# Attention with scores, softmax and values in one loop, without the running maximum

## The reference

```python
xn = _layernorm(x)                       # x: 2 x 8192 x 1024
q, k, v = xn @ Wq, xn @ Wk, xn @ Wv      # 1024 x 1024 each
scores = where(causal, -inf, q @ k.T)
s = softmax(scores / sqrt(1024)) @ v
g = silu(ffn(xn))                        # gate, up: 1024 -> 3072, down: 3072 -> 1024, integer weights
x = x + s * g
```

## Time and profile before

| | us |
|---|---|
| median of 2 runs | 2159.85 (2154.26 to 2165.43) |
| the profiled execution | 2145.53 |
| its span, on core 7, the slowest | 2143.8 |
| spans of the eight cores | 2132.1 to 2143.8 |
| attention, first to last matmul, on core 7 | about 1404 to 2126 |

### The profile page before, as it was taken

One profiled execution on the slowest core, in us unless ns is written; L12 is line 12 of the kernel. 1 busy time (PEld: TensorE's weight loads), 2 busy tenths in 40 slices (PEclk: granted clock), 3 DMA queues, 4 the chain that ended last, 5 costly groups with the idle time before them and its releaser, 6 DMA issues.

```text
span 2143.8 us, 24577 instructions; the slowest of 8 cores (2132.1 to 2143.8 us)
## 1 busy us (share of the span) xinstructions
PE 1677.2 (78%) x8544; PEld 797.7 (37%) x8544; DVE 534.8 (25%) x1356; ACT 551.3 (26%) x842; POOL 87.3 (4%) x149
## 2 busy tenths in 40 slices
PE   0232499999999986799989998966778687878875
PEld 0222344444444443344434443323333333333332
DVE  3000033443443342111001110033323242341430
ACT  0242543444344333011001110022222222221321
POOL 0000000000000000000000000000000000001000
PEclk9955599999999998899999999988889999989988
DMA  9999333342433331433102330077787685765834
GB/s 194 199 217 192 107 136 138 138 156 102 155 138 141 115 118 61 120 76 79 40 1 56 73 79 10 1 248 222 234 258 236 217 273 200 244 235 185 295 138 157
DMA packets 165751, 320.66 MB, mean 150 GB/s; under 512 B 105088, under 2 KB 111232, under 8 KB 143104
## 3 DMA queue, kind: packets, MB, share of 16 engines
q0 software_dynamic: 29968, 151.00, 24.6%
q1 hardware_dynamic: 124144, 149.20, 22.6%
q10 hardware_dynamic: 11520, 18.88, 2.5%
HBM read 283.41 MB, written 60.82 MB: 161 GB/s over the span
## 4 chain that ended last, share of the span: by engine, by line
PE 65%; DMA 18%; ACT 5%; another core or an unknown queue 4%; issue 3%; DVE 2%; ACTq 1%; SPq 1%; DVEq 0%; POOL 0%; POOLq 0%
PE psBC L405 10%; DMA vbuf<-vv_s 9%; PE psD L592 8%; PE psA L550 8%; PE psA L435 5%; PE psD L435 5%; PE psA L667 4%; PE psBC L800 4%; PE psD L800 4%; PE psD L560 4%; PE psBC L560 4%; PE psBC L461 3%; DMA kbuf<-kT_s 3%; DMA wst<-wu 2%
## 5 line engine op out<-in xcount | busy, mean ns | idle before, releaser
L405 PE MATMUL psBC<-xns,wk_b 128*128 128x512 bf16 x1024 | 225.3, 381 | 1.3 <-ACT xns L381 1.3
L250 PE MATMUL psA<-ident_b,wst 128*128 128x128 bf16 x576 | 69.5, 295 | 189.9 <-DMA wst<-wg 86.9
L550 PE MATMUL psA<-xnq,wgu 128*128 128x512 bf16 x768 | 175.9, 383 | 27.5 <-DMA wgu<-wuT_s 27.5
L800 PE MATMUL psBC<-vbuf,pT 128*128 128x512 bf16 x512 | 138.5, 419 | 70.7 <-DMA vbuf<-vv_s 63.8
L592 PE MATMUL psD<-wdT_b,hact 128*128 128x512 bf16 x768 | 170.0, 381 | 21.4 <-ACT g_b L601 17.7
L360 DVE TENSOR_SCALAR xnr<-xkb,mvall,rstdall 128x1024 bf16<-128x1024 f32 x80 | 61.6, 810 | 500.5 <-PE psA L372 498.4
L667 PE MATMUL psA<-kbuf,qT 128*128 128x512 bf16 x608 | 143.0, 393 | 25.7 <-DMA kbuf<-kT_s 17.6
L800 PE MATMUL psD<-vbuf,pT 128*128 128x512 bf16 x576 | 143.1, 395 | 6.0 <-DMA vbuf<-vv_s 6.0
L405 PEld LDWEIGHTS psBC<-xns,wk_b 128*128 128x128 bf16 x1024 | 100.6, 98 | 123.2 <-issue 3.7
L775 ACT ACTIVATE pT<-psA 128x1024 bf16<-128x1024 bf16 x72 | 69.5, 976 | 261.6 <-PE psA L763 261.6
L250 PEld LDWEIGHTS psA<-ident_b,wst 128*128 128x128 bf16 x576 | 52.9, 133 | 206.2 <-issue 206.1
(11 more groups left out here) (83 smaller groups left out, 1677.3 us busy)
## 6 DMA issues: line engine op xcount, KB each, us to landing
vbuf<-vv_s POOLq DMA_DIRECT2D x72, 1024.0 KB, 5.8
kbuf<-kT_s SPq DMA_DIRECT2D x40, 1024.0 KB, 9.8
xkb<-xk SPq DMA_DIRECT2D x16, 2048.0 KB, 10.9
kbufX<-kT_s SPq DMA_DIRECT2D x32, 1024.0 KB, 13.6
kT_s<-kst POOLq DMA_DIRECT2D x16, 1024.0 KB, 5.7
vv_s<-vst POOLq DMA_DIRECT2D x16, 1024.0 KB, 4.1
wgu<-wgT_s SPq DMA_DIRECT2D x48, 256.0 KB, 3.0
wgu<-wuT_s SPq DMA_DIRECT2D x48, 256.0 KB, 3.5
```

What stands on the lines that cost most here:

```text
L250: wfree=wfree, hpar=hpar: t.transpose(trA[:, par * 1024 + (rb - r0) * 128: par * 1024 + (rb - r0 + 1) * 128], wstf[:, hpar * 12288 + rb * ...
L405: (lambda t, dcc=dcc, pb=pb, e=e, ph=ph: t.matmul(psBC[:, ph * 512:(ph + 1) * 512], wk_b[:, dcc, e * 128:(e + 1) * 128], xns[:, pb, dcc, : ...
L550: gb=gb: t.matmul(psA[:, gb + sh * 512:gb + (sh + 1) * 512], wgu[:, par, 0, dcc, :], xnq[:, dcc, qs + sh * 512:qs + (sh + 1) * 512], start ...
L800: ph=ph, tgt=tgt, nv=nv: t.matmul(tgt[:, eh * 512:(eh + 1) * 512], pT[:, ph, sl, kt, :], vbuf[:, ph, kt, eh * 512:(eh + 1) * 512], start=( ...
```

## The change

The two parts of a pair become one loop over the blocks. In round s, SyncE loads K(s), GpSimd loads V(s), and TensorE does the transposes of s-1, QK of s and AV of s-1, in this order; after the last block come its transposes and its AV. The scores have two banks (`psA`, the first 1024 columns) in place of eight, the transposes the other half of `psA`. The per-block maximum, its scaling, the maximum over the blocks, the factors and the rescaling are left out: ScalarE computes `Exp(score/32)` directly. The mask is still added by VectorE in the last block of each tile. The combine of tile A waits for A's last AV only, that of B for B's. Sizes and numbers of the matmuls, transposes and transfers stay as they are.

```diff
-            for sup in range(nsupB):
...
-                    E.qsop("v", lambda v, bk=bk, sl=sl, sup=sup: v.reduce_max(
-                        msb[:, sl, sup:sup + 1], score_ap(bk),
-                        axis=AX.X, negate=True))
...
-                        func=AF.Exp, bias=msb[:, sl, sup:sup + 1],
...
-                        v.tensor_scalar_mul(
-                            pbufs[sl][:, sup * 512:(sup + 1) * 512],
-                            pbufs[sl][:, sup * 512:(sup + 1) * 512],
-                            fsb[:, sl, sup:sup + 1]))
...
+            def emit_tr(s):
+                tb = 2048 + (s % 2) * 1024
+                slots = slots_of(s)
                 for sl in slots:
+                    E.qwait("t", "a", exp_m[(sl, s)])
+                fw = trb_free.get(s % 2)
+                if fw is not None:
+                    E.qwait("t", "a", fw)
...
+            def emit_av(s):
+                ph = s % 2
+                E.qwait("t", "a", pte_m[s])
+                E.qwait("t", "vbuf%d" % ph, vdma_m[s])
+                if s == 0:
+                    for bw in obank_free:
+                        E.qwait("t", "v", bw)
+                    del obank_free[:]
...
+            for s in range(nsupB):
...
+                kdma = E.mark("kbuf%d" % ph4)
+
+                vph = s % 2
+                vw = vread_m.get(vph)
+                if vw is not None:
+                    E.qwait("pl", "t", vw)
...
+                vdma_m[s] = E.mark("vbuf%d" % vph)
+
+                if s >= 1:
+                    emit_tr(s - 1)
+
+                slots = slots_of(s)
+                E.qwait("t", "kbuf%d" % ph4, kdma)
+                for sl in slots:
+                    fw = score_free.get(sl)
+                    if fw is not None:
+                        E.qwait("t", "a", fw)
...
+                if s >= 1:
+                    emit_pte(s - 1)
+
+                E.qwait("a", "t", qk_m)
+                if s == 0:
+                    E.qwait("a", "v", lin_prev[0])
...
+                        func=AF.Exp, scale=1.0 / 32.0,
...
+                if s >= 1:
+                    emit_av(s - 1)
+
+            emit_tr(nsupB - 1)
+            emit_pte(nsupB - 1)
+            emit_av(nsupB - 1)
```

More of the change, by code:

```diff
@@ L703, in build @@
[L703 to L712, removed]
@@ L730, in build @@
[L730 to L738, removed]
@@ L740, in q_transpose @@
[L740 to L775, removed]
@@ L803, in q_av @@
                                 vbuf[:, ph, kt, eh * 512:(eh + 1) * 512],
-                                start=(vb == 0 and kt == 0),
-                                stop=(vb == nv - 1 and kt == 3)))
-                av_tm.append(E.qgroup("t", fns, "t"))
-                vbuf_last[ph] = av_tm[-1]
-                pt_last[ph] = av_tm[-1]
-            pend = None
[L811 to L814, removed]
-                pend = stx
@@ L816, in build @@
-            q_av(pend)
-            E.qwait("v", "t", av_tm[-1])
+                                start=(s == 0 and kt == 0),
+                                stop=(s == nv - 1 and kt == 3)))
+                av_m[s] = E.qgroup("t", fns, "t")
+                vread_m[ph] = av_m[s]
+                pt_last[ph] = av_m[s]
+            for s in range(nsupB):
+                ph4 = s % 4
+                kb_t = kbuf if ph4 < 2 else kbufX
+                kb_ap = kb_t[:, ph4 % 2, :, :]
+                kb_w = kbuf_last.get(ph4)
+                if kb_w is not None:
+                    E.qwait("sy", "t", kb_w)
+                E.qdma("sy", "kbuf%d" % ph4, lambda s_, sup=s, kb_ap=kb_ap:
+                       s_.dma_start(
+                           out=kb_ap,
+                           in_=kT_s[sup].rearrange("p (c q) -> p c q",
+                                                   q=512)))
+                kdma = E.mark("kbuf%d" % ph4)
[3 more added lines that the diff above has]
+                    E.qwait("pl", "t", vw)
+                E.qdma("pl", "vbuf%d" % vph, lambda g, sup=s, vph=vph:
+                       g.dma_start(
+                           out=vbuf[:, vph, :, :],
+                           in_=vv_s[sup].rearrange("p (t e) -> p t e",
+                                                   e=DM)))
+                vdma_m[s] = E.mark("vbuf%d" % vph)
[7 more added lines that the diff above has]
+                        E.qwait("t", "a", fw)
+                fns = []
+                for sl in slots:
+                    kk = kA if sl == 0 else kB
+                    for e in range(DC):
+                        fns.append(lambda t, e=e, kk=kk, sl=sl, kb_t=kb_t,
+                                   php=ph4 % 2: t.matmul(
+                            psA[:, sl * 512:(sl + 1) * 512],
+                            qT[:, e, kk * 128:(kk + 1) * 128],
+                            kb_t[:, php, e, :],
+                            start=(e == 0), stop=(e == DC - 1)))
+                qk_m = E.qgroup("t", fns, "t")
+                kbuf_last[ph4] = qk_m
+                msk_m = {}
+                for sl in slots:
+                    if s == (nsupA if sl == 0 else nsupB) - 1:
+                        E.qwait("v", "t", qk_m)
+                        msk_m[sl] = E.qsop("v", lambda v, sl=sl:
+                                           v.tensor_tensor(
+                            psA[:, sl * 512:(sl + 1) * 512],
+                            psA[:, sl * 512:(sl + 1) * 512],
+                            maskb[:], ALU.add))
+                if s >= 1:
[3 more added lines that the diff above has]
+                    E.qwait("a", "v", lin_prev[0])
+                for sl in slots:
+                    if sl in msk_m:
+                        E.qwait("a", "v", msk_m[sl])
+                    exp_m[(sl, s)] = E.qsop("a", lambda a, sl=sl, sup=s:
+                                            a.activation(
+                        out=pbufs[sl][:, sup * 512:(sup + 1) * 512],
+                        in_=psA[:, sl * 512:(sl + 1) * 512],
+                        func=AF.Exp, scale=1.0 / 32.0,
+                        accum_out=lsb[:, sl, sup:sup + 1]))
+                    score_free[sl] = exp_m[(sl, s)]
+                if s >= 1:
+                    emit_av(s - 1)
@@ L819, in build @@
+            emit_tr(nsupB - 1)
+            emit_pte(nsupB - 1)
+            emit_av(nsupB - 1)
+            E.qwait("v", "a")
+            for sl, nsup in ((0, nsupA), (1, nsupB)):
+                E.qsop("v", lambda v, sl=sl, nsup=nsup: v.reduce_sum(
+                    lsum[:, sl:sl + 1], lsb[:, sl, 0:nsup], axis=AX.X))
+            lin_prev[0] = E.qsop("v", lambda v: v.reciprocal(linv[:],
+                                                            lsum[:]))
             for sl, kk in ((0, kA), (1, kB)):
+                av_last = av_m[(nsupA if sl == 0 else nsupB) - 1]
+                E.qwait("v", "t", av_last)
```

133 lines of the change are left out of this document (35 added, 98 removed).

## The result

The changed kernel takes 2073.05 us in the median (11 runs), against 2154.02 us for the kernel before (10 runs). The ratio is 0.963, 95% interval 0.9605 to 0.9655: 3.7% faster, where 5.4% was forecast (2043 us against 2159.85). The profiled execution took 2071.9 us, its span on core 7 is 2070.1 us.

A forecast was written before the change was run, and what follows sets the result against it. TensorE's 501 us of full-clock matmuls and transposes were taken as the attention stage's need; pair 1's end at 1423.3, plus 490, plus 98 for boundaries, gave 2011.5 against 2126, hence 2043 us for the kernel, range 2000 to 2105.

The forecast's parts named there:

- What bounds the kernel, 501 us at full clock: Attention stage: matmuls and transposes need 501 of 722 us at full clock; 168 us are idle, 53 lower clock.
- (1): Maximum, factors and rescaling go: the 8 TensorE holes, one per pair (55.4 us of waits for the rescaling), vanish.
- (2): Inside a pair, Exp runs under AV(s-1) and the copy under QK(s): no holes; without cover up to 1.65 us per block.
- (3): Loads inside a pair: each V load has 11.3 us, demand is 285 GB/s against 341 available; cost 0.
- the rival of a transfer-bound loop: Third rival: the loop becomes bound by transfers, 168 MB at 230 GB/s taking 730 us; no gain, 2150 us, chance 0.07.
- the slower one: Fourth rival: V's own queue is the limit at 189 GB/s, 888 us for 168 MB; kernel 2320 us, chance 0.04.
- (4): Start of pairs 2 to 8: TensorE waits 9.4 us for V(0) (bounds 2.3 and 17.2); 14.05 us per boundary, together 98.
- Taking turns: Pair boundary: V's queue moves 2.6 MB at half rate while K loads, a wait of some 12 us for V(0).
- The clock behind it: After each V(0) wait, the first matmuls run at a lowered clock: 1.7 to 3 us, 2.0 taken.
- stage clock 0.95 or more: Sign that the prediction is right: mean granted clock of the attention stage at 0.95 or more, against 0.91 before.
- (5): Pair 1, first of the attention stage: last AV ends at 1423.3 us; before, pair 2 began at 1429.5.
- (6): Tail after the last AV: A's combine has already begun, 1.6 us less.

The follow-up runs named there:

- the loop across pairs: Changed kernel with four V buffers, V(0) to V(3) loaded ahead of stores and input tiles, and the loop carried across pairs: ratios 0.9202 and 0.9189 to the kernel before.

## Why the prediction was right, and what it had too small

- **What bounds the kernel, 501 us at full clock.** Right. Blocks for both tiles follow each other every 7.35 us (1949 to 2045 us in pair 8), where 7.37 was worked out. The transposes before took 0.92 us per block at half clock, by the difference of their starts, and not the 1.2 read from the earlier trace rows; no term of the sum uses it.
- **(1) the holes vanish.** Right, but it counted them as gain without asking what landed in them. It had looked at pair 8, where the transfer engines stand still in the hole; in pairs 2 to 7 they are full. Alone it is worth 17 us of 2142, not the 34 to 49 expected of it; only with the loop does the rest come.
- **(2) cover inside a pair.** Right: no wait for Exp or the copy in mid-pair. It was even larger than thought: it hides the block maximum too, but for the blocks with the mask.
- **(3) V inside a pair costs 0.** Nearly: 6.1 us in 3 waits, all at the last block of a pair, whose load is issued just before the K loads for the next pair; about half of that would have been waits for the copy. In mid-pair the two queues move 280 GB/s at a share of 0.78, as worked out, and neither the rival of a transfer-bound loop nor the slower one happened.
- **(4) the wait for V(0).** The mechanism, the place and the count (7) were right. Its size was the mis-sized term: 9.4 us taken, 13.0 measured, 25 of the 35 us by which the stage came out longer (642 against 607). The issue was at Z+5.3, a little earlier than the Z+6.4 worked out; the landing took 13.9 to 17.1 us at the seven boundaries (16.9 in pair 8), where I had taken 12.1, from the load of pair 1 at the start of the stage. That row was the wrong neighbour. At a boundary four K loads for the next pair have been issued just before, and two more come beside V(0); with those two held, V(0) lands in 9.4 to 11.6 us. The rows that resembled it were those of V(0) at the seven boundaries before, 17.9 to 27.5 us. The prediction used the one of pair 8, 19.9, as its upper bound, and called them all "12 us or more". That its bounds hold the measured value is therefore partly luck: by my estimate the mean of the seven, 23.5 us, would have given a wait of 20.8 us and 2123 us, outside the range.
- **Taking turns.** The Trainium skill ("DMA: Bandwidth & Descriptors", section "Queues, rings and completion order") says that a transfer engine takes turns between the queues that have work for it. The prediction's estimate from it was a wait of some 12 us; 13.0 were measured, and the earlier landing with K held agrees with it. The rule was at hand and left out of the sum. The fit that the Trainium skill's same page has (section on the anatomy of one DMA, SWDGE path) gives an estimate of 4.4 us for such a load. No V load here reached it: the shortest took 5.0 us, the shortest V(0) at a boundary of the changed kernel 13.9.
- **The clock behind it:** 1.6 to 2.6 us, 2.1 in the mean of the seven, 2.0 taken. TensorE's busy time beyond 501 is 24 us, where about 18 had been counted. The sign "stage clock 0.95 or more" did not come true: 0.91, as before. The granted clock is low in the holes themselves; with the holes nearly gone (the loop across pairs) it is 0.97.
- **(5) pair 1:** 20.7 us, 18.9 predicted. **(6) tail:** about 1.3 us, 1.6 predicted.
- **What lies ahead of the stage** took 6.6 us more on core 7 in the profiled execution of the changed kernel (its first QK at 1411.0, before at 1404.4), 1.8 of it the first K load. On the other seven cores the start moved by -3.3 to +2.1 us, and within one execution it differs by up to 8 us between cores. It belongs to no term of the change.

The forecast was 114.5 us for the stage, and 80 were measured. Of the 35 us between, 25 are the wait for V(0); the rest is about 3 for V at the last block of a pair, 2 in pair 1 and some 6 for the clock.

## What to carry to other kernels

When two phases become one loop, follow the first load of each round in its issuing list: what stands ahead of it, what else has just been issued on the other queues, and how many buffers let it start early. A load's landing time is to be taken from the rows with the same traffic around it, all of them, and not from the one with the same neighbours in its own queue. Before a hole is counted as gain, look in every round at what the transfer engines do in it. Loads that are not needed soon should not be issued next to one that is; and before a reduction is removed to save time, look whether the loop hides it.

## What the runs showed that I had not expected

- Exp without a bias takes 0.60 us for 128x512, with the maximum as bias 0.69. First the changed kernel (pair 8), then the one with the maximum (pair 4):

```profile
1930.09 0.60 ACT L764 ACTIVATE pbufA<-psA 128x512 bf16<-128x512 f32 x1 [2.37 <-PE psA L736]
```

```profile
1564.99 0.69 ACT L775 ACTIVATE pbufA<-psA,msb 128x512 bf16<-128x512 f32 x1 [3.50 <-DVE msb L761]
```

- While one core stood waiting for V(0), its transfers ran at 398 GB/s for 5 us (1930 to 1935), above the 341 of the earlier trace rows.
- The kernel with more waits (K held) was 38 us faster, and the one with more work (the block maximum) was not slower.
